# Wide attention: one feed-forward chunk inside each score unit, transposes and context in one bank, sums behind the next unit's maxima

## The reference, cut to what matters

```python
def _L2_xattn_ref(x, context, mask, ...):
    xn, cn = layer_norm(x, ln_g, ln_b), layer_norm(context, cln_g, cln_b)
    q = xn @ Wq                       # 16 heads of 64
    k, v = split(cn @ Wkv)            # one head of 64, shared by all
    sim = q @ k.T * 64 ** -0.5 + mask
    out = (softmax(sim) @ v) @ Wout
    a, gate = split(xn @ W1)          # 512 each
    return out + (a * silu(gate)) @ W2
x = x + tanh(g_xattn[2]) * _L2_xattn_ref(_layernorm(x), ctx_1024, mask_BxSxS2_ff0, ...)
```

## Time and profile before

| what | us |
|---|---|
| median of 3 runs (1269.73 to 1273.92) | 1269.73 |
| the profiled execution's own time | 1267.3 |
| its span, from first to last instruction | 1265.5 |
| PE busy in the span | 1084.6 (86%) |
| DVE busy | 676.5 (53%) |
| ACT busy | 463.2 (37%) |
| POOL busy | 338.2 (27%) |

### The profile page before, as it was taken

The page is one execution under the profiler, slowest core; times in us unless marked ns, Lnnn a source line. Parts: engine busy times, 40 slices in busy tenths (PEclk is TensorE's granted clock), DMA queues, the critical chain, the costliest instruction groups (busy, mean ns, idle before and its releaser), DMA issues.

```text
span 1265.5 us, 25823 instructions
## 1 busy us (share of the span) xinstructions
PE 1084.6 (86%) x10082; PEld 915.3 (72%) x10082; DVE 676.5 (53%) x1560; ACT 463.2 (37%) x1005; POOL 338.2 (27%) x312
## 2 busy tenths in 40 slices
PE   5998988988799997979897887879699979889894
PEld 4666776766689987868576787757699957767783
DVE  3734745447566747372663646446565636355462
ACT  2634625426234333232341232325233345154231
POOL 1021035120251545121122410130432452341422
PEclk9998968989889996979896788889799989689697
DMA  9100001000152340000000100000022230010032
GB/s 340 43 1 1 2 1 52 2 1 2 25 181 71 85 175 16 2 1 1 1 2 7 44 2 1 1 1 2 19 77 82 62 127 15 1 35 2 30 91 73
DMA packets 54038, 52.99 MB, mean 42 GB/s; under 512 B 6816, under 2 KB 49312, under 8 KB 53024
## 3 DMA queue, kind: packets, MB, share of 16 engines
q1 hardware_dynamic: 48800, 40.85, 10.0%
q0 software_dynamic: 5120, 10.50, 2.9%
HBM read 34.02 MB, written 17.30 MB: 41 GB/s over the span
## 4 chain that ended last, share of the span: by engine, by line
PE 76%; DVE 11%; POOL 6%; issue 4%; ACT 2%; DMA 1%; SPq 1%; DVEq 0%; POOLq 0%
PE bank L1577 12%; PE bank L1589 7%; PE bank L509 5%; PE bank L498 5%; PE bank L327 5%; PE bank L290 4%; PE bank L873 3%; PE bank L307 3%; PE bank L485 3%; POOL small L365 2%; PE bank L836 2%; PE bank L318 2%; PE bank L476 2%; PE bank L911 2%; PE bank L894 2%
## 5 line engine op out<-in xcount | busy, mean ns | idle before, releaser
L365 POOL TENSOR_TENSOR small<-small,neghalf 128x4 f32<-128x4 f32 x56 | 56.5, 1018 | 501.1 <-DVE small L387 326.0
L1577 PE MATMUL bank<-xTs,qx 128*128 128x128 f32 x1160 | 160.9, 287 | 8.7 <-DVE qx L1648 5.0
L1577 PEld LDWEIGHTS bank<-xTs,qx 128*128 128x128 f32 x1160 | 144.7, 198 | 20.2 <-issue 15.6
L1263 POOL DMA_INDIRECT yg<-ybuf,posi x80 | 77.9, 973 | 180.8 <-DMA ybuf<-otx 153.9
L663 DVE TENSOR_REDUCE mx<-bank 128x8 f32<-128x512 f32 x128 | 88.1, 689 | 63.1 <-PE bank L485 60.9
L1589 PE MATMUL bank<-wmoe,otx 128*128 x764 | 106.8, 277 | 4.2 <-DVE otx L1677 2.7
L580 ACT ACTIVATE probsT<-bank 128x512 f32<-128x512 f32 x128 | 73.5, 597 | 84.9 <-PE bank L498 82.0
L498 PE MATMUL bank<-csb,probs 128*128 128x128 f32 x512 | 80.7, 289 | 22.9 <-ACT probs L584 22.9
L1589 PEld LDWEIGHTS bank<-wmoe,otx 128*128 128x128 f32 x764 | 95.1, 192 | 5.7 <-issue 5.3
L1237 POOL DMA_INDIRECT xbuf<-rows,posi x80 | 80.3, 1004 | 66.7 <-DVE ebi L1224 37.4
L290 PE MATMUL bank<-warm_x,warm_w 128*128 128x224 bf16 x588 | 97.2, 275 | 0.0
(11 more groups left out here) (266 smaller groups left out, 1976.6 us busy)
## 6 DMA issues: line engine op xcount, KB each, us to landing
ybuf<-otx SPq DMA_DIRECT2D x122, 64.0 KB
xblk<-xbuf SPq DMA_DIRECT2D x26, 256.0 KB
wmoe<-in_w_moe SPq DMA_DIRECT2D x3, 2048.0 KB, 10.0
wmoe<-in_w_moe SPq DMA_DIRECT2D x1, 3072.0 KB, 11.6
xbuf<-otx SPq DMA_DIRECT2D x2, 1472.0 KB, 20.4
wmoe<-in_w_moe SPq DMA_DIRECT2D x1, 1536.0 KB, 14.8
xbuf<-rows,posi POOLq DMA_INDIRECT x80, 2.2
yg<-ybuf,posi POOLq DMA_INDIRECT x80
```

The costliest lines, as they stand in the source:

```text
L365: g.tensor_tensor(s.col(1)[:, at:at + PC], s.col(0)[:, at:at + PC], neghalf[:, 0:PC], ALU.pow)\
L1263: nc.gpsimd.indirect_dma_start(yg[:, p % 2, k, i, :], None, ybuf[g].ap(), bass.IndirectOffsetOnAxis(ap=posi[g][:, j:j + 1], axis=0)).then_ ...
L1577: mm = pe.matmul(U[half][:, ch * P:(ch + 1) * P], w[:, 0:P], xTs[:, na % 3, :], start=True, stop=True)
```

## The change: what it does

- The feed-forward chunks move into the units. Chunk `k` is now made in `OY` at unit `k` by PE, ACT and DVE, each chunk waiting until DVE is done with the one before.
- `OY` is free for that since the context of a unit now goes to `TP`, where its transposes have been: the transposes of unit `k` wait until ACT has copied the context of unit `k` - 1 out.
- `project` and the feed-forward's second matmul (now `shrink`) accumulate in `SB`, begin once DVE has read the last scores out, and are spread over the last two units.
- The next call's `queries(1)`, which write `SB`, wait for the new `x`; before, its value projection waited.
- On DVE the sums and inverses of unit `k` - 1 stand between the maxima of unit `k` and their subtraction; before, they stood behind it.
- The slots at the end of a call are gone, on all engines.

```diff
--- before.py
+++ after.py
@@ -838,12 +838,12 @@
                 mm.then_inc(*c.give("big_proj_q"))
 
             queries(0)
+            if j > 0:
+                pe.wait_ge(*c.next("x_new"))
             queries(1)
             if j == 0:
                 pe.wait_ge(*c.next("normed"))
             pe.matmul(OY[:, 0:T], Wt("kx"), cn, start=True, stop=True).then_inc(*c.give("big_proj_k"))
-            if j > 0:
-                pe.wait_ge(*c.next("x_new"))
             w, a = weight_at("vx")
             for b in range(BT):
                 for half in (0, SEQ):
@@ -882,65 +882,68 @@
                 pe.wait_ge(*c.next("big_probs_normed"))
                 if u == 0:
                     pe.wait_ge(*c.next("big_v_blocks"))
+                else:
+                    pe.wait_ge(*c.next("contextT_taken"))
                 for b in range(BT):
                     mm = pe.transpose(TP[:, b * P:(b + 1) * P], s.probs[:, u % 2, b * P:(b + 1) * P], C("ident"))
                 mm.then_inc(*c.give("big_probsT"))
 
             def weigh(u):
                 pe.wait_ge(*c.next("probsT_taken"))
-                if u >= 1:
-                    pe.wait_ge(*c.next("contextT_taken"))
                 for b in range(BT):
-                    mm = pe.matmul(OY[:, b * P:(b + 1) * P], s.vdiag[:, b, :], s.probsT[:, u % 2, b * P:(b + 1) * P],
+                    mm = pe.matmul(TP[:, b * P:(b + 1) * P], s.vdiag[:, b, :], s.probsT[:, u % 2, b * P:(b + 1) * P],
                                    start=True, stop=True)
                 mm.then_inc(*c.give("contextT"))
 
             def hidden(ch):
-                if ch >= 2:
+                if ch >= 1:
                     pe.wait_ge(*c.next("big_hidden_done"))
-                else:
-                    pe.wait_ge(*c.next("big_added"))
-                S = (SA, SB)[ch % 2]
-                pe.matmul(S[:, 0:T], Wt("ffx", 2 * ch), xn, start=True, stop=True)
-                pe.matmul(S[:, T:], Wt("ffx", 2 * ch + 1), xn, start=True, stop=True)\
+                pe.matmul(OY[:, 0:T], Wt("ffx", 2 * ch), xn, start=True, stop=True)
+                pe.matmul(OY[:, T:], Wt("ffx", 2 * ch + 1), xn, start=True, stop=True)\
                   .then_inc(*c.give("ff_hidden"))
 
             def project(u):
                 for c2 in range(2):
                     rhs = s.otx[:, u, :].rearrange("p (b c q) -> p b c q", b=BT, c=2)[:, :, c2, :]
-                    pe.matmul(TP[:, 0:T], Wt("ox", 4 * (u % 2) + 2 * (u // 2) + c2), rhs, start=(u + c2 == 0),
-                              stop=False)
+                    mm = pe.matmul(SB[:, 0:T], Wt("ox", 4 * (u % 2) + 2 * (u // 2) + c2), rhs,
+                                   start=(u + c2 == 0), stop=(u == 3 and c2 == 1))
+                return mm
+
+            def shrink(ch):
+                pe.matmul(SB[:, 0:T], Wt("ff2x", ch), s.fact[:, ch, :], start=False, stop=False)
 
             for k in range(6):
                 if k == 0:
                     scores(0)
+                elif k == 1:
+                    hidden(1)
+                else:
+                    weigh(k - 2)
                 yield
                 if k == 1:
                     scores(1)
-                if k >= 2:
-                    weigh(k - 2)
-                if k == 5:
-                    hidden(1)
-                yield
-                if k == 4:
-                    hidden(0)
+                elif k < 4:
+                    hidden(k)
+                elif k == 4:
+                    pe.wait_ge(*c.next("big_added"))
+                    pe.wait_ge(*c.next("big_added"))
+                    project(0)
+                    for ch in range(3):
+                        shrink(ch)
+                else:
+                    project(2)
+                    pe.wait_ge(*c.next("big_hidden_done"))
+                    shrink(3)
                 yield
                 if 1 <= k < 5:
                     transposes(k - 1)
-                yield
-            for ch in (2, 3):
-                project(ch - 2)
-                hidden(ch)
-                yield
-            project(2)
-            pe.wait_ge(*c.next("contextT_taken"))
-            project(3)
-            for ch in range(4):
-                if ch >= 2:
-                    pe.wait_ge(*c.next("big_hidden_done"))
-                mm = pe.matmul(TP[:, 0:T], Wt("ff2x", ch), s.fact[:, ch, :], start=False, stop=(ch == 3))
-            mm.then_inc(*c.give("projected"))
-            yield
+                elif k == 5:
+                    pe.wait_ge(*c.next("contextT_taken"))
+                    project(3).then_inc(*c.give("projected"))
+                yield
+                if k == 4:
+                    project(1)
+                yield
 
         def wide_act(s, c, p, j):
             a = nc.scalar
@@ -959,31 +962,27 @@
 
             def hidden(ch):
                 a.wait_ge(*c.next("ff_hidden"))
-                a.activation(s.fx[:, ch % 2, :], (s.SA, s.SB)[ch % 2][:, T:], ACT.Tanh, scale=0.5)\
+                a.activation(s.fx[:, ch % 2, :], s.OY[:, T:], ACT.Tanh, scale=0.5)\
                  .then_inc(*c.give("ff_hidden_tanh"))
 
             for k in range(6):
                 yield
-                yield
-                if k < 4:
-                    a.wait_ge(*c.next("big_shifted"))
-                    a.activation(s.probs[:, k % 2, :], s.probs[:, k % 2, :], ACT.Exp).then_inc(*c.give("big_exped"))
                 if k == 2 and p < 2 and j == 0:
                     wait_stored(a, 0, 1)
                 if k >= 2:
                     a.wait_ge(*c.next("contextT"))
-                    a.activation(s.otx[:, k - 2, :], s.OY[:, :], ACT.Copy).then_inc(*c.give("contextT_taken"))
-                yield
+                    a.activation(s.otx[:, k - 2, :], s.TP[:, :], ACT.Copy).then_inc(*c.give("contextT_taken"))
+                yield
+                if k < 4:
+                    hidden(k)
+                yield
+                if k < 4:
+                    a.wait_ge(*c.next("big_shifted"))
+                    a.activation(s.probs[:, k % 2, :], s.probs[:, k % 2, :], ACT.Exp).then_inc(*c.give("big_exped"))
                 if 1 <= k < 5:
                     a.wait_ge(*c.next("big_probsT"))
                     a.activation(s.probsT[:, (k - 1) % 2, :], s.TP[:, :], ACT.Copy).then_inc(*c.give("probsT_taken"))
-                if k >= 4:
-                    hidden(k - 4)
-                yield
-            for ch in (2, 3):
-                hidden(ch)
-                yield
-            yield
+                yield
 
         def wide_dve(s, c, p, j):
             dve = nc.vector
@@ -1022,11 +1021,10 @@
                    .then_inc(*c.give("big_shifted"))
 
             def hidden(ch):
-                S = (s.SA, s.SB)[ch % 2]
                 dve.wait_ge(*c.next("ff_hidden_tanh"))
                 link(c, dve.scalar_tensor_tensor(out=s.fx[:, ch % 2, :], in0=s.fx[:, ch % 2, :], scalar=1.0,
-                                                 in1=S[:, T:], op0=ALU.add, op1=ALU.mult))
-                dve.scalar_tensor_tensor(out=s.fact[:, ch, :], in0=s.fx[:, ch % 2, :], scalar=0.5, in1=S[:, 0:T],
+                                                 in1=s.OY[:, T:], op0=ALU.add, op1=ALU.mult))
+                dve.scalar_tensor_tensor(out=s.fact[:, ch, :], in0=s.fx[:, ch % 2, :], scalar=0.5, in1=s.OY[:, 0:T],
                                          op0=ALU.mult, op1=ALU.mult).then_inc(*c.give("big_hidden_done"))
 
             def normed(k):
@@ -1040,25 +1038,20 @@
                 if k < 4:
                     added(k)
                 yield
+                if 1 <= k < 5:
+                    normed(k - 1)
+                yield
                 if k < 4:
                     shifted(k)
                 yield
-                if 1 <= k < 5:
-                    normed(k - 1)
-                yield
-                if k >= 4:
-                    hidden(k - 4)
+                if k < 4:
+                    hidden(k)
                 yield
             c.skip("big_probsT", 2)
-            for ch in (2, 3):
-                hidden(ch)
-                yield
             dve.wait_ge(*c.next("projected"))
-            dve.scalar_tensor_tensor(out=x, in0=s.TP[:, 0:T], scalar=tg[:, 2:3], in1=x, op0=ALU.mult,
+            dve.scalar_tensor_tensor(out=x, in0=s.SB[:, 0:T], scalar=tg[:, 2:3], in1=x, op0=ALU.mult,
                                      op1=ALU.add).then_inc(*c.give("x_new"))
             yield
-
-
 
         def route_pe(s, c, l, kind, src, after, gate):
 
```

More of the change, by code:

```diff
@@ L966, in wide_act @@
                 yield
+                if k == 2 and p < 2 and j == 0:
+                    wait_stored(a, 0, 1)
+                if k >= 2:
+                    a.wait_ge(*c.next("contextT"))
+                    a.activation(s.otx[:, k - 2, :], s.TP[:, :], ACT.Copy).then_inc(*c.give("contextT_taken"))
+                yield
+                if k < 4:
+                    hidden(k)
                 yield
@@ L970, in wide_act @@
```

(6 more changed lines are left out.)

## The result

The change takes **1240.7 us** in the median of four runs (1236.55 to 1241.54), the kernel before 1269.73 (1268.28 to 1273.92): a ratio of 0.976, 95% interval 0.973 to 0.979. The forecast was 1234.5 in a range of 1226 to 1252. The profiled execution of the change took 1236.55 us, its span is 1234.7.

The account below looks back on a forecast made before the run. Bound by PE in the first and last legs, PE-DVE hand-overs between. Round 37.06 + 16.71 + 1.5 = 55.3 us instead of 64.07; four save 35.2, giving 1232.1, plus 2.4 for the median: 1234.5 us, range 1226 to 1252.

Parts of the forecast that it names:

- Leg 1: Round start to DVE's first score read-out: keeps 11.53 us; the earlier wait for the new x costs nothing.
- Leg 2: First read-out to unit 2's transposes: paced by DVE's queue, chunks included, 24.43 us, plus 1.10 from POOL's start to the transposes.
- Units 1 and 2 at 7.31 each: DVE's time per middle unit: maxima 2.89, sums and inverses 1.61, subtractions 1.21, chunk 1.60 us.
- the sentence that costs the order of sums and maxima at nothing: DVE's new order within a unit adds no time; it only keeps DVE from waiting for the exponentials.
- Its own sign for this: The prediction's stated test: DVE's queue step is wrong if a unit differs much from 7.31 us with DVE full.
- The three things that must fit into a unit: Within 7.31 us: context copy before transposes 4.77, PE's work 4.54, POOL's gathers with two multiplications 6.8 us.
- Leg 3: Unit 2's transposes to round end: PE's queue of contexts, projections, shrink matmuls and transposes, 16.71 us at full clock.
- one stretch at low clock: Allowance of 1.5 us per round for PE running at 0.55 clock for 3.41 us at the round's end.
- The sum: A round of 55.3 us instead of 64.07; four rounds save 35.2 us, profiled execution 1232.1 us.
- Rival 1: Clock stays up throughout: round 53.8 us, total 1228.5 us; chance 0.73 together with the forecast.
- Rival 2: The second scores, scores(1), again at half rate delay unit 2's transposes: round 60.3 us, total 1254.5 us; chance 0.1.
- Rivals 3 and 4: PE at half rate: pacing the units, 1248.5 us, chance 0.1; or throughout the last leg, 1295.5 us, chance 0.04.

Follow-up runs that it names:

- the experiment with the small multiplication: The change with POOL's multiplication cut to one head of eight (64 of 512 columns), the rest left unnormalised: 1230.73 us, one run.
- the swap alone: The kernel before with only DVE's sums and inverses moved ahead of the next unit's subtraction: 1274.34 us, ratio 1.0025.

## Why the prediction came out as it did

The direction, the size and the mechanism held; one term of the sum was too small.

- *Leg 1, 11.53 us, and the earlier wait for the new `x` at nothing.* Right: 11.53 in three of the four rounds, and the query matmuls of the next stream follow without a gap. The third round's took 693.89 - 681.90 = 11.99, at clock 0.96; its calls have `j` = 0 and wait for no new `x`, so this is no cost of the wait.
- *Leg 2 becomes DVE's queue.* Right: DVE has no wait of over 0.5 us between the first read-out and the last inverse, and the chain runs through it. Unit 0 took 479.57 - 473.48 = 6.09 (forecast 6.11), POOL's start to the transposes 501.39 - 500.30 = 1.09 (forecast 1.10). At this cut the kernel before took 26.75 in its first round, so the forecast's 25.53 was a saving of 1.2 in this leg, and what came was a loss of 1.2.
- *Units 1 and 2 at 7.31 each.* **This is the step that failed**, in its term for the subtractions, 1.21 us from the earlier trace rows. It measured 2.34, so that a unit is 8.41. With it fell the sentence that costs the order of sums and maxima at nothing: that order is what sets the subtraction beside POOL's multiplication. The row for the term was taken from a place where POOL did nothing of the kind, and the working didn't ask what POOL does at the new place. Its own sign for this came: a unit that takes much more than 7.31 with DVE full. Both units make 2.2 of the 2.38 us by which leg 2 exceeds 25.53. Over the four rounds the second legs (27.91, 27.91, 27.92, 27.90) are 9.5 us over.
- The Trainium skill, "SBUF — State Buffer", section "Who interferes with whom", states this collision: a VectorE instruction with two inputs in SBUF contends with a GpSimd instruction that reads SBUF; what they share is an exclusive lock, and the order of issue decides who is blocked. The rounds agree: 1.21 turned into 2.34 and, in the experiment with the small multiplication, 0.29 into 0.63. The prediction didn't weigh it; it cites a rule on the clock alone.
- *The three things that must fit into a unit.* Right. Transposes waited for POOL (2.39, 1.17 and 0.79 us), never for the copy of the context, and POOL's gathers ended ahead of its next multiplication, with 0.78 us to spare at unit 2 and 0.38 at unit 3.
- *Leg 3, 16.71 us, and 1.5 for one stretch at low clock.* This leg begins at unit 2's transposes, so its like in the kernel before is 25.36, and not the 18.72 of the earlier trace rows that the prediction sets beside it. The sum, 18.2, was slightly high: 17.16, 18.38, 18.38 and 17.17, 1.7 us less in all. At clock 1.00 it is 17.16, because the second stream's transposes start 1.45 us after the first's, where 1.00 is usual: POOL's stretched second multiplication again. The low clock came in two of the four rounds (0.91 in those legs) and cost 18.38 - 17.16 = 1.2.
- *The sum.* For the four rounds it was 256.27 - 35.2 = 221.1, and they took 229.30, 8.2 more: 9.5 over in leg 2, 0.5 over in leg 1, 1.7 under in leg 3. The untouched part was 3.8 us shorter, by scatter, so that the profiled execution missed its 1232.1 by only 4.4, which is luck; the median of runs stands 4.15 above that execution, where 2.4 were reckoned.
- *Rival 1*, the clock up throughout at 53.8 a round, did not come true in the change: its second legs ran at 0.88 to 0.94. The kernel with the small multiplication comes near its time (53.67 in the first round, at clock 1.00; 54.1 in the mean of four). That it comes so near is in part luck, since 0.75 of it is saved on POOL; without that the first round would be 54.4, an estimate, and the 53.8 some 0.6 low but for the collision.
- *Rival 2*, the second scores at half rate: no. They took 3.79 us at 480.84, full rate, and the same in the other three rounds, with chunk 1's matmuls directly ahead of them, as the argument against it had it.
- *Rivals 3 and 4*, PE at half rate in the units or in leg 3: no. PE waits for POOL in the units, and leg 3 ran at 0.91 or 1.00. The low stretches of the second leg lie beside DVE's full queue. The Trainium skill's rule of "TensorE: Matmul & The Clock Gate" that the prediction cited, on short groups that cycle through banks, agrees with what is left below 1.00 there, 0.88 to 0.94. But the clock of that leg rose by the change, from 0.68, and the rule decided no time: the four second legs are equal to 0.02 us.

## What to carry to other kernels

A duration from the trace holds for the neighbours that it had there: before an operation is moved, look up what the other engines do at its new place, and above all whether DVE with two SBUF operands comes beside GpSimd. Such a meeting can stand in another stage of the same trace already, as below. An order that costs nothing while its engine has waits (the swap alone: 1.0025) becomes a bound once the waits are filled. And where the whole program scatters by 5 us, cut the stages that are touched out of the span and compare those sums: they gave 6.5 and 6.7 us for the order where medians gave 4.9 or 9.5.

## What was not expected of the hardware

Two 128x512 subtractions on DVE and two multiplications of that size on POOL, 1.29 and 2.04 us alone, took 2.41 and 2.49 when they met, from 483.46 to 486.49 together: 3.03 us, not far from their sum. The same held against POOL's sum of gathered rows, 1.27 to 1.72 where the subtraction had started first, and unchanged where POOL had. Reductions, and operations with one operand in a bank, were not touched by POOL's multiplication (0.63 and 0.37 to 0.42 us beside it).

The subtraction's second operand is a broadcast, but that is not what it takes. The trace of the kernel before has the same meeting in another stage, at a line that the prediction doesn't look at: L1159 subtracts one column of an SBUF tile from another, with no broadcast, in 0.17 us; beside POOL's additions to `xs` it took 0.71 and 1.25.

```profile
170.98 0.17 DVE L1159 TENSOR_TENSOR gap<-top 128x4 f32<-128x4 f32 x1
...
661.90 1.25 DVE L1159 TENSOR_TENSOR gap<-top 128x4 f32<-128x4 f32 x1
```

POOL's timeline beside it:

```profile
661.87 2.47 POOL L1144 TENSOR_TENSOR xs<-xs,upd 128x512 f32<-128x512 f32 x2
```

The first of the two additions took 1256 ns, from 661.87 to 663.13, and L1159 ended at 663.15. So the collision could have been seen in the trace that the prediction had.

Two SBUF operands are not the whole condition, and no run here explains the rest. A cast with one SBUF input (L1163, 0.18 us alone) took 0.65 beside the same additions. And L1217, a multiplication of two SBUF tiles (0.22 us alone), began 0.29 us into a POOL operation of 1.57 us (L369, which adds a value per partition to `xs`), took 0.47 and was done 0.8 us before it; the next one took 0.21 while that operation still ran.

```profile
183.48 1.57 POOL L369 TENSOR_SCALAR xs<-xs,bog 128x512 f32<-128x512 f32 x1
...
183.77 0.61 DVE L1217 TENSOR_TENSOR prod<-pick,rk 128x64 f32<-128x64 f32 x2
```
